# A sorted mixture-of-experts kernel: zeros written at the start, last tiles that end at an expert's last row, rows in pairs, and all result transfers begun by ACT

## The reference

```python
# x: 16 sequences of 512 tokens, 256 wide
x = x + 0.5 * ffn(layernorm(x))
x = x + attention(layernorm(x))      # 16 heads of 16, ALiBi bias, 8 heads look back, 8 ahead
x = x + 0.5 * ffn(layernorm(x))      # the same weights again

def ffn(flat):                       # a mixture of experts
    out = two shared experts, 128 wide: silu(x wg_s) * (x wu_s) @ wd_s
    probs = softmax(flat @ router_w)                   # 16 experts
    weights, indices = top_k(probs, 2); weights /= weights.sum()
    return out + sum over the two chosen experts e of
        weight[e] * (silu(x wg_r[e]) * (x wu_r[e])) @ wd_r[e]    # 64 wide
```

## Time and profile before

| | us |
|---|---|
| median of 3 runs | 2260.67 (2259.05 to 2264.02) |
| the profiled execution | 2255.13 |
| its span, first to last instruction | 2253.3 |

### The profile page before, as it was taken

One profiled execution on the slowest core, in us unless ns is written; L12 is line 12 of the kernel. 1 busy time (PEld: TensorE's weight loads), 2 busy tenths in 40 slices (PEclk: granted clock), 3 DMA queues, 4 the chain that ended last, 5 costly groups with the idle time before them and its releaser, 6 DMA issues.

```text
span 2253.3 us, 35352 instructions
## 1 busy us (share of the span) xinstructions
PE 1702.2 (76%) x10696; PEld 1121.1 (50%) x10696; DVE 1474.2 (65%) x3920; ACT 1046.5 (46%) x2263; POOL 947.3 (42%) x999
## 2 busy tenths in 40 slices
PE   3758875678788888886877889888887677985382
PEld 2646655446455555543544546555554334553251
DVE  4765666677766657676677776766787757573432
ACT  3325543354455555554454555645554335553151
POOL 2643337454423231445444343443545635234604
PEclk8979996789999999988998989999998789997686
DMA  7468753645867666555449765666746686864895
GB/s 206 139 205 248 251 182 97 121 90 154 227 180 211 187 193 172 151 96 124 92 75 239 182 171 146 178 167 138 176 105 132 207 247 164 244 188 149 265 310 162
DMA packets 327979, 392.80 MB, mean 174 GB/s; under 512 B 40296, under 2 KB 269032, under 8 KB 327784
## 3 DMA queue, kind: packets, MB, share of 16 engines
q1 hardware_dynamic: 269520, 284.59, 48.4%
q0 software_dynamic: 24576, 67.14, 10.5%
q10 hardware_dynamic: 33696, 38.81, 5.2%
HBM read 188.58 MB, written 155.19 MB: 153 GB/s over the span
## 4 chain that ended last, share of the span: by engine, by line
PE 29%; DMA 26%; DVE 17%; issue 10%; POOL 10%; SPq 4%; ACT 3%; another core or an unknown queue 0%; ACTq 0%; DVEq 0%; POOLq 0%
DMA sorted_x<-xn,position 7%; DMA y_tok<-sorted_y,position 6%; DMA den<-o_store 4%; PE bank L1202 3%; PE bank L1098 3%; PE bank L991 3%; PE bank L1109 3%; PE bank L993 3%; PE bank L992 3%; PE bank L1182 2%; POOL sorted_x L1737 2%; DMA q_stack<-shift_t 2%; DVE x_att L1646 2%; PE bank L1215 2%; POOL y_tok L1763 2%
## 5 line engine op out<-in xcount | busy, mean ns | idle before, releaser
L1343 ACT ACTIVATE p_buf<-bank 128x512 f32<-128x512 f32 x640 | 361.8, 599 | 264.4 <-PE bank L1182 212.1
L1574 DVE TENSOR_REDUCE row_max<-bank 128x1 f32<-128x512 f32 (+2 forms) x768 | 349.2, 504 | 76.4 <-PE bank L1165 70.6
L1737 POOL DMA_INDIRECT sorted_x<-xn,position x224 | 221.4, 988 | 232.6 <-DMA sorted_x<-xn,position 140.4
L1797 POOL TENSOR_SCALAR_AFFINE_SELECT p_buf<-p_buf 128x512 f32<-128x512 f32 x256 | 161.6, 645 | 316.5 <-ACT p_buf L1343 314.9
L1182 PE MATMUL bank<-q_stack,k_stack 101*128 101x512 bf16 (+3 forms) x1024 | 244.7, 318 | 57.2 <-DMA q_stack<-shift_t 46.6
L1149 PE MATMUL bank<-k_stack,q_stack 99*128 99x512 bf16 (+3 forms) x1024 | 254.2, 319 | 32.4 <-issue 19.6
L1763 POOL DMA_INDIRECT y_tok<-sorted_y,position x192 | 185.5, 966 | 213.2 <-DMA y_tok<-sorted_y,position 117.0
L1202 PE MATMUL bank<-p_buf,v_rows 128*32 128x512 f32 (+3 forms) x2048 | 197.5, 485 | 91.0 <-POOL p_buf L1797 88.0
L1309 ACT ACTIVATE t_y<-bank 128x256 f32<-128x256 f32 x406 | 133.3, 380 | 156.4 <-PE bank L1109 137.4
L991 PE MATMUL bank<-w_down,hs_buf 128*128 128x256 f32 x256 | 89.1, 348 | 126.5 <-POOL hs_buf L1770 125.4
L1676 DVE RECIPROCAL den<-den 128x128 f32<-128x128 f32 x128 | 110.0, 913 | 101.2 <-DMA den<-o_store 99.8
(11 more groups left out here) (193 smaller groups left out, 3910.7 us busy)
## 6 DMA issues: line engine op xcount, KB each, us to landing
t_w<-expert_w SPq DMA_DIRECT2D x137, 256.0 KB
t_x<-sorted_x SPq DMA_DIRECT2D x137, 256.0 KB
sorted_y<-t_y SPq DMA_DIRECT2D x137, 256.0 KB
q_stack<-qk_part SPq DMA_DIRECT2D x192, 128.0 KB
k_stack<-qk_part SPq DMA_DIRECT2D x192, 128.0 KB
sorted_x<-zeros SPq DMA_DIRECT2D x69, 256.0 KB, 3.6
p_buf<-expert_w SPq DMA_DIRECT2D x66, 256.0 KB
p_buf<-sorted_x SPq DMA_DIRECT2D x66, 256.0 KB
```

The source lines that it names most:

```text
L1343: act.activation(p_of(u), psum("score", *of)[:, :], ACT.Exp).then_inc(*exp_done.step(*of))
L1574: ins = dve.tensor_reduce(row_max[g % 2][:, n:n + 1], src[:, col:col + q1 - q0], X, ALU.max)
L1737: pool.indirect_dma_start(sorted_x[l, group_of(l, b)], bass.IndirectOffsetOnAxis(ap=position[:, b, k, t:t + 1], axis=0), xn[buffer][:, t, ...
L1797: pool.affine_select(blocks, blocks, [[0, GH], [1 if ahead else -1, P]], ALU.is_ge, zero, base=0, channel_multiplier=-1 if ahead else 1).t ...
```

## The change

- The fills go. For each group SP begins one transfer, which writes zeros to the first 256 rows of all 16 regions; the planner gives it the key -0.9 for the first group (right behind the expert weights, -1.0) and 19, 24, 29 and 34 for the others (the loads of batch rows 2 to 5 have 9.7, 17.7, 25.7 and 33.7). The scatters of a group wait for it. The zeros lie in `rest[0]`, which attention uses later and which therefore waits for all five.
- If an expert has more than 256 rows, its last tile begins earlier, so that it ends at the expert's last row; some rows are then computed twice. `table` computes how many rows earlier, and `find` corrects the positions in such a tile too: its operations have 8 x 32 columns, and `table` has eight more small operations, three of them ahead of the tiles' rows.
- The piece "tile put" goes. ACT begins the transfers of the results in all groups, right after its copy.
- In the transfers of these rows partition p holds the rows 2p and 2p + 1, so that each piece in HBM is 2 KB.
- The table no longer waits for the previous group's fills, and the tiles no longer wait for theirs.

```diff
     def tile(at, l, g, j, pace=1.0):
-        fills = [(("fill", l, g), "SP")] + ([(("fill", l, g), "ACT")] if many_tiles(l, g) else [])
-        part(at - 2.5, "SP", 0.8, x, *fills, *sent, *last,
+        part(at - 2.5, "SP", 0.8, x, (("table", l, g), "DVE"), *sent, *last,
...
-        if many_tiles(l, g):
-            part(at + 1.0 * pace, "ACT", 1.5, made, (made, "PE"),
-                 takes=[("t_y", ("t_y", l, g, j), [(made, "ACT landed")])], lag=3.5)
-        else:
-            part(at + 1.0 * pace, "ACT", 0.8, made, (made, "PE"),
-                 takes=[("t_y", ("t_y", l, g, j), [(put, "SP landed")])])
-            part(at + 2.0 * pace, "SP", 0.57, put, (made, "ACT"), lag=3.0)
+        part(at + 1.0 * pace, "ACT", 1.5, made, (made, "PE"),
+             takes=[("t_y", ("t_y", l, g, j), [(made, "ACT landed")])], lag=3.5)
...
+    for n, (l, g) in enumerate(ALL_GROUPS):
+        part(-0.9 if n == 0 else 14 + 5 * n, "SP", 0.7, ("fill", l, g), lag=14.0)
...
     def sort(at, l, g):
-        if many_tiles(l, g):
-            part(at + 0.1, "SP", 10.4, ("fill", l, g), (("table", l, g), "DVE"), *old, lag=4.0)
-            part(at + 0.1, "ACT", 10.4, ("fill", l, g), (("table", l, g), "DVE"), *old, lag=4.0)
-        else:
-            part(at + 0.1, "SP", 20.8, ("fill", l, g), (("table", l, g), "DVE"), *old, lag=4.0)
...
             def rows(t, row):
-                return t[bass.ds(row, RT), :].rearrange("(i p) d -> p i d", p=P)
+                return t[bass.ds(row, RT), :].rearrange("(p i) d -> p i d", i=2)
...
                 elif name == "fill":
                     l, g = of
-                    sp.wait_ge(*table_step.at(l, g, "fill"))
-                    for e in range(0, E, 2 if many_tiles(l, g) else 1):
-                        row = sp.value_load(fill_i[0:1, e:e + 1])
-                        sp.dma_start(rows(sorted_x[l, g], row), zeros[:, :].unsqueeze(1).broadcast_to((P, 2, D))
-                                     ).then_inc(*filled.step(l, g, e))
+                    sp.dma_start(
+                        sorted_x[l, g][0:SPARE].rearrange("(e c) d -> e c d", e=E)[:, 0:RT, :]
+                        .rearrange("e (p i) d -> p e (i d)", i=2),
+                        zeros[:, :].unsqueeze(1).broadcast_to((P, E, 2 * D))).then_inc(*filled[l, g].step())
...
-                    if many_tiles(l, g):
-                        act.wait_ge(*ty_out.at(*of, 1))
-                        act.dma_start(put_rows(*of), t_y[i][:, :, :]).then_inc(*ty_put_act[i].step(*of))
+                    act.wait_ge(*ty_out.at(*of, 1))
+                    act.dma_start(put_rows(*of), t_y[i][:, :, :]).then_inc(*ty_put_act[i].step(*of))
...
+                done("rest", dve.scalar_tensor_tensor(early, tiles, float(RT), n_of, ALU.mult, ALU.subtract))
+                done("early", dve.scalar_tensor_tensor(early, n_of, float(RT), early, ALU.is_gt, ALU.mult))
+                done("its own", dve.scalar_tensor_tensor(early_rows[:, :], end, tile_no, early,
+                                                         ALU.is_equal, ALU.mult))
+                done("both", dve.tensor_tensor(past, past, early_rows[:, :], ALU.subtract))
...
                 done("past", dve.scalar_tensor_tensor(
-                    beyond[:, :, :], at.unsqueeze(2).broadcast_to((P, 2 * NT, E)), -float(CAP),
-                    region.unsqueeze(1).broadcast_to((P, 2 * NT, E)), ALU.add, ALU.is_ge))
+                    beyond[:, :, :], at.unsqueeze(2).broadcast_to((P, 2 * NT, 2 * E)), 0.0,
+                    bound[l, g][:, :].unsqueeze(1).broadcast_to((P, 2 * NT, 2 * E)), ALU.add, ALU.is_ge))
...
+                    if (b, m, w) == (0, 0, 0):
+                        dve.wait_ge(spare_in, 16 * len(ALL_GROUPS))
+                        for key in ALL_GROUPS:
+                            dve.wait_ge(*filled[key].at())
...
                     if n == 0:
                         pool.wait_ge(*place_step.at(l, b, "position"))
+                        pool.wait_ge(*filled[l, group_of(l, b)].at())
```

More of the change, by code:

```diff
@@ L329, in routing @@
             some = [(("scatter", l, b, n - d), "POOL landed")] if n >= d else []
-            part(at[3] + 0.01 * n, "POOL", 1.25, ("scatter", l, b, n), (position, "DVE"), *some, lag=2.2)
+            part(at[3] + 0.01 * n, "POOL", 1.25, ("scatter", l, b, n), (position, "DVE"), (("fill", l, group_of(l, b)), "SP"),
+                 *some, lag=2.2)
     def shared(at, l, b):
@@ L513, in schedule @@
                 part(t + at + 0.3 * w, "ACT", 0.69, qk, (qk, "PE"))
-                part(t + at + 0.3 * w, "DVE", 0.75, qk, (qk, "ACT"))
+                part(t + at + 0.3 * w, "DVE", 0.75, qk, (qk, "ACT"), *[(("fill", *of), "SP landed") for of in ALL_GROUPS])
                 part(t + at + 0.6 + 0.1 * w, "ACT", 0.62, rest, (qk, "DVE"))
@@ L652, in build @@
         tile_i = {(l, g): sb(f"tile_i{l}{g}", [P, 2], I32) for l, g in ALL_GROUPS}
-        fill_i = sb("fill_i", [P, E], I32)
-        unused = {(l, g): sb(f"unused{l}{g}", [P, E]) for l, g in ALL_GROUPS}
-        beyond = placed[:, :, :, :].rearrange("p k t e -> p (k t) e")
+        three = [[sb(f"{n}{i}", [P, 2 * E]) for i in range(min(3, len(ALL_GROUPS)))] for n in ("bound", "nearer")]
+        bound, nearer = ({of: some[n % 3] for n, of in enumerate(ALL_GROUPS)} for some in three)
+        early_rows = sb("early_rows", [P, E])
         beyond_rows = sb("beyond_rows", [P, 2 * NT])
-        zeros = sb("zeros", [P, D])
+        zeros = rest[0]
         row_max = [sb(f"row_max{i}", [P, GH * NT]) for i in range(2)]
@@ L897, in do @@
                                  ).then_inc(*tw_in[i].step(*of))
-                elif name == "tile put":
-                    l, g, j = of
-                    sp.wait_ge(*ty_out.at(*of, 1))
-                    sp.dma_start(put_rows(*of), t_y[index["t_y", l, g, j]][:, :, :]).then_inc(*ty_put(*of).step(*of))
                 elif name == "gather":
@@ L1535, in table @@
                                   ).then_inc(*table_step.step(l, g, "row"))
+                dve.tensor_scalar(bound[l, g][:, 0:E], region, float(CAP), None, ALU.add
+                                  ).then_inc(*table_step.step(l, g, "behind"))
+                done("last", dve.scalar_tensor_tensor(bound[l, g][:, E:2 * E], tiles, float(RT), region,
+                                                      ALU.mult, ALU.add))
+                done("last one", dve.tensor_scalar(bound[l, g][:, E:2 * E], bound[l, g][:, E:2 * E], float(-RT), None,
+                                                   ALU.add))
+                done("left", dve.tensor_tensor(left, left, early, ALU.add))
+                dve.tensor_scalar(early, early, -1.0, None, ALU.mult).then_inc(*table_step.step(l, g, "nearer"))
             def find(l, b):
```

57 lines of the change are left out of this document (19 added, 38 removed).

## The result

The changed kernel took 2279.1 us (median of 4 runs, 2276.4 to 2283.7) beside 2260.5 for the kernel before (4 runs, 2259.1 to 2264.0): a ratio of 1.0083, interval 1.0045 to 1.0121. It is 18.6 us slower, where I had forecast 2245.1, 15.6 us faster. The time lies inside my range and on the other side of no change. The profiled execution took 2280.1, its span is 2278.4.

A forecast was written before the change was run, and what follows sets the result against it. No engine was full; the chain mixed PE 29%, DMA 26%, DVE 17%, POOL 10%, ACT 3%. Terms +14 - 4.8 - 18 + 3.6 - 3 + 4.6 - 4 - 8 = -15.6 us gave 2245.1 us, range 2214 to 2280.

The forecast's parts named there:

- The start, +14: First stage: zeros for all five groups ahead of loads, put and scatters cost 14 us, between 0 and +30.
- The prediction's estimate of 11.6 us for a fill: Start: 2 us plus bytes over 436 GB/s gives 11.6 us a fill instead of 12.6; sum 1 us better.
- The first sort, -4.8: First sort: removing the block of fills gives -7, six wider corrections cost +2.2; together -4.8 us.
- The three sorts in the middle, -18: Middle sorts: removing SP's 16 fills gives 6 us each, -18 in all, between 0 and -51.
- Corrections and tables, +2.2 and +4.6: DVE: six wider corrections at the first sort, +2.2; 26 more and five tables elsewhere, 17.6 us at 26%, +4.6.
- Puts, +3.6 and -3: 137 puts moved from SP: ACT's 55 us of issue at 6.5% cost +3.6; SP's relief gives -3.
- Rival 1: ACT's puts decide: all 55 us of issue gives 2296 us, slower than 2265 from 44% on; chance 0.20.
- Pairs, -4: Tile loads and stores: 2 KB pieces instead of 1 KB move faster, -4 us, between 0 and -25.
- The last sort, -8: Last sort: without 4.19 MB of zeros scattered and fetched rows come earlier, -8 us, between 0 and -12.6.
- Rival 2: Start takes back what the sorts give: fills hold up loads and puts, +30, 2261 us, no change; chance 0.17.

The follow-up runs named there:

- fills_only: Kernel before, its order kept, with fills at the start, last tiles ending at the last row and wider corrections; single rows, SP's puts: 2283.0 us, ratio 1.0106.
- zeros_twice: weights_later plus the same 21 MB of zeros also written at the start in 1 KB pieces, everything at the sorts unchanged: 2272.4 us, ratio 1.0041.
- more_finds: weights_later with DVE work added: two operations of every correction done twice, one of every table nine times: 2262.1 us, ratio 0.9993.
- puts_only: Kernel before, same order, with ACT instead of SP beginning the puts of the middle groups: 2265.7 us, ratio 1.0038.
- fills_spread: fills_only with loads of rows 2 to 5 ahead of the first fill, the other fills spread over the first stage, and pairs: 2273.2 us, ratio 1.0062.
- weights_later: Kernel before with rows in pairs and expert weights loaded behind the loads of batch rows 2 to 5: 2241.4 us (0.9920); run again, 2245.0 (0.9944).
- plan_only: Kernel before, with the planner told that ACT's copy of a result costs 1.5 instead of 0.8 us: 2266.9 us, ratio 1.0023.
- order_new: Kernel before's fills and corrections, with ACT's puts, pairs and the changed kernel's order on every engine: 2284.1 us, ratio 1.0101.
- fills_late: fills_spread with only the first group's zeros at the start, the others copied in DRAM later, at 107 to 1115 us: 2269.9 us, ratio 1.0049.

## Why the prediction was wrong, step by step

**The start, +14: right in kind, too small.** The step said that row 2's first rows land near 51 instead of 38.6, with a wait of 25 us on DVE; they came at 49.6 with 23.6. What was missed is the next sentence's "its zeros have landed by 50": the scatters' own zeros had, but the other groups' zeros were then on the engines, and eight scatters took 18 us instead of 10. So +20 at row 6, which the new order mostly made up by 477 us, and which the old order kept (+19 at the first mark of attention in fills_only). I also called the stretch from 40 to 100 us the emptiest. It was, but its scatters wait for one another's landing, and bytes beside them cost 24 us in zeros_twice (15 to 33). By the Trainium skill ("DMA: Bandwidth & Descriptors", Issuing engines are not separate DMA queues), whose rule I had used only for the puts, POOL's scatters share the 16 engines with SP's zeros; the runs agree, with 8 us more for eight scatters of 128 KB. The prediction's estimate of 11.6 us for a fill stays untested: the five fills took 19.4 us from issue to landing (median), each among other transfers.

**The first sort, -4.8: it gave nothing.** My -7 for the block of zeros fell. The chain of the kernel before through this stretch (start, length, what):

```profile
123.77 3.54 issue
...
135.44 4.54 another core or an unknown queue
140.01 0.69 DVE q_stack L1616
...
144.72 0.30 DVE placed L1550
...
151.80 0.69 DVE h_buf L1604
```

and that of fills_only, where no engine has a block there:

```profile
144.50 6.42 issue
...
157.42 0.69 DVE q_stack L1623
158.11 2.12 another core or an unknown queue
...
165.30 0.43 DVE beyond L1557
...
174.77 0.69 DVE h_buf L1611
```

From row 7's statistics (117.21 and 137.94) to the first correction it is 27.5 us with the block and 27.4 without: as DVE's wait shrank from 4.54 to 2.12, the step of issue ahead of it grew from 3.54 to 6.42. SP does load the first tile's rows earlier, as the step wanted, 26.8 us after row 7's statistics instead of 34.6; but PE comes to that tile 46.0 us after them instead of 44.1. The six corrections then take 9.5 us instead of 7.1, +2.4, and that was my +2.2. So -4.8 was about +2.

**The three sorts in the middle, -18: nothing.** In fills_only, whose order is that of before, the marks around the second sort (475 to 699 us before) lie 4.5 us further apart, around the third (1109 to 1290) 0.3 further, around the fourth (1752 to 1885) 0.3 nearer. SP stood for 15.7 to 18.8 us, but what was due behind it seems to have been wanted no sooner; the chain of before goes through scatters, PE and DVE there. These stretches also hold 23 of the longer corrections and three tables, some 15 us of DVE's work, so a few us that the sorts gave may be hidden in the sum. I had counted a third of a blocked queue's time with one step of 4.33 us to show for it.

**Corrections and tables, +2.2 and +4.6: the work was right, the price open.** DVE's work: 19.8 us forecast, 18.6 more in the profile. Its price by more_finds is 53% instead of 26%, so some 10 us instead of 6.8; but 26% lies in that run's interval. Chain time over busy time is a mean, and the six corrections above stand in the chain one behind the other.

**Puts, +3.6 and -3: mis-sized.** Alone they cost 8.6 us (2 to 15). Rival 1 was right in kind, at 16% of the 55 us of issue and far from the 44% from which it would have decided. The wait by which I would have known it, POOL for exponentials, did grow by tens of microseconds. Over the whole span, first the kernel before, then the changed one, then puts_only (total, times, longest):

```profile
POOL p_buf L1797 <- ACT p_buf L1343: 314.9, 82, 13.6
```

```profile
POOL p_buf L1793 <- ACT p_buf L1322: 341.9, 85, 11.5
```

```profile
POOL p_buf L1794 <- ACT p_buf L1340: 328.7, 83, 13.4
```

By that sign the rival would have been right, so it was a poor sign: it counts a wait, and not what the wait delays. PE's wait for what POOL makes of the exponentials did not grow (88.0 us before, 86.0 after). Nor is it what grew most where the changed kernel loses most, in rows 8 to 11. Two lines of the waits there, 1291 to 1706 us:

```profile
POOL p_buf L1793 <- ACT p_buf L1322: 86.6, 25, 8.1
ACT t_y L1289 <- PE bank L1099: 58.1, 19, 12.2
```

Over the same rows of the kernel before the first is 77.8 and the second 19.3. In the new order ACT, in order, stands 39 us more for tiles whose product PE has not finished. These rows lose 32 us; that the one is the cause of the other was not tried.

**Pairs, -4: right**, -7.5 and -1.4 alone (each give or take 6).

**The last sort, -8: half.** In fills_only two of DVE's lines answer to the waits of 12.6 and 10.7 us in the earlier trace rows:

```profile
2158.22 0.42 DVE L1557 SCALAR_TENSOR_TENSOR beyond<-position,bound 128x256 f32<-128x256 int32 x1 [5.67 <-DMA sorted_x<-xn,position]
...
2186.37 0.48 DVE L1653 SCALAR_TENSOR_TENSOR x_ffn<-q_stack,share,x_ffn 128x256 f32<-128x256 f32 x1 [7.89 <-DMA q_stack<-sorted_y,position]
```

From the last batch row's ranks to that second line it is 45.9 us instead of 49.8 (2103.97 to 2153.79): -3.9. POOL's issue and three longer corrections are next, as the step feared.

**The sum.** For the zeros and corrections the terms made -12 and the runs +24. Taken apart at an equal start order: bytes at the start +24, DVE's work +13, both with the sorts' zeros gone +28 (fills_spread against weights_later). So what is left for leaving out the fills at all five sorts is a gain of 8 or 9 us, give or take 13 (5 or 6 with DVE's work at the changed kernel's size), where I had counted 33 (7, 18 and 8). That is the step that failed, most of all its -18 for the middle: SP's blocked queue and the full engines stood there, and the chain hardly went through them. It is a remainder; the traces of the five sorts above (nothing, nothing, 3.9) say the same. The second step is the start, priced at +14 where its bytes cost 24. Rival 2 said it in words (the start takes back what the sorts give) but let the sorts give what I had forecast. The planner's order, which I left without a price, moved the time by +5 (plan_only), by some -10 (with the zeros) and by some +18 (order_new less the puts and pairs), each with the interval given above: it can't be added to the rest.

Open remain the 15 us or so by which fills_late is above DVE's share. Its bytes stood in other places and were copied in DRAM, so they may cost as much elsewhere as at the start. The last tiles that begin earlier, which are in fills_only, fills_spread and fills_late alike, were not tried alone and may have a share. Open is also why the new order loses in rows 8 to 11.

## What to carry to other kernels

A stretch in which the DMA engines are idle is not free when its work is a chain of single transfers: here scatters wait for one another's landing, and 21 MB put beside them cost 24 us. Before a blocked queue or a full stretch is priced, look at what would be next on the chain without it: here other waits took the place of the one that went, and 33 us of expected gain were 8 or 9. And look at the queue ahead of the first awaited transfer: four loads put in front of copies that nobody awaits gave 10 us of the 14.5 that the best version gains.

## What was not expected of the hardware

With the DMA engines full, SP stood 10.7 us for a load that it had issued in 1.9, and 3 to 5 us for one instruction of 4 MB. The time that SP stands for an issue is thus no fixed cost: it grew more than fivefold beside 345 GB/s, most of it zeros. The put of row 0, 0.37 us on SP before, took 6.3. And 21 MB written through engines that were 40 to 57% busy cost 24 us of the whole time. At the 333 GB/s of the earlier trace rows they are 63 us of the engines' time, and weights_later leaves them idle for 51 us between 36 and 140 (24 x 0.60 + 40 x 0.49 + 40 x 0.43), so a part of the 24 us may be that the bytes do not fit; the scatters' waits above begin before the engines are full (79 and 87% busy up to 100 us).
